# An adaLN transformer block: other places for a batch's products, GpSimd's small works and unread products, and another order at both ends

## The chip, the cores and the metric

One core of a Trainium2 chip runs the whole program. The metric is the device time of one execution in microseconds. TensorE does the matrix products, VectorE, ScalarE and GpSimd the elementwise work, SyncE's queue issues nearly all DMAs. Here GpSimd is called POOL in rows, VectorE DVE, ScalarE ACT, TensorE PE.

## The reference

Eight batches of 512 tokens, width 128, 16 heads of 8, all in f32. Only what the kernel's stages answer to is kept:

```python
mod = (silu(c) @ wmod).reshape(8, 6, 1, 128)       # sa, ca, ga, sb, cb, gb
ga = (2 * (ga >= 0) - 1) * maximum(abs(ga), 0.25)  # gb likewise
h = layernorm(x) * (1 + ca) + sa
q, k, v = split(h @ w_qkv.T)                       # 16 heads
a = q @ k.T * 8 ** -0.5
a = a - max(a, axis=-1)
s = where(a >= 0, 1 + a * (1 + a/2 * (1 + a/3)), 1 / (1 - a * (1 - a/2 * (1 - a/3))))
x = x + ga * ((s / sum(s)) @ v @ w_out.T + b_out)
h = layernorm(x) * (1 + cb) + sb
h = 2 * relu(s0 * [h, -h] @ sign(k0))              # 512 wide
h = 2 * relu(s1 * h @ sign(k1))                    # 512 wide
x = x + gb * (s2 * h @ sign(k2))
```

## The kernel before

**Steps.** The attention of all batches is one pipeline of 128 steps, 16 a batch (`b`, `n` in the code); 16 steps ahead (batch FIRST, -1) and 5 behind fill and drain it. In a step m, TensorE makes the maximum-shifted logits of group m+1 as two pairs of products into the two halves of PSUM tensor Z (`scores`, line 561), and for group m+7 unshifted logits into SA (`logits`, line 576), of which VectorE takes row maxima (line 975). ScalarE squares Z (line 720), VectorE makes a cubic of square and Z (line 966), POOL squares that (line 1201), ScalarE takes its reciprocal square root two steps later (`prob_of`, line 734): that is the unnormalised probability. Five steps behind, it is multiplied with v into OP (`with_v`, line 593); each fourth step OP is copied to OT and from there DMAs gather numerators and denominators into nd. Every fourth step (n = 1, 5, 9, 13) VectorE also does three small operations on the maxima (`of_maxima`), whose rows go to QH by eight small DMAs.

**Products in between.** All other products stand in the tables MISC (lines 68 to 97): name, which batch relative to b, and pieces (step, place, number of chunks). Places in a TensorE step (`pe_step`): scores 0, **a**, logits 1, fill, with_v, **b**, scores 1, **c**, logits 0, **d**. For batch b these are hT, q, k, v of b+1, x1, h2T and l0_0 to l0_3 of b-1, l1_0 to l1_3 and y of b-2. They share the one PSUM bank MB but for those in `own_bank`; the first chunk of each waits until the product before it has been copied out, by ScalarE (`take`, at the place of the product's last piece, after the squares or after prob), or for the late ones by VectorE (`take_late`). Batches 0 and 1 have no l1 and y, batch 0 also no x1, h2T and l0.

**Products without reader.** `fill` (line 612) multiplies ident by a block of W1 into MB in the steps of table FILL; nothing reads it. The entry names the product whose copy must be over.

**Small works.** MAIN_AT gives the steps of the work on x1: xbg (x plus gate times bias), woG (output weights times gate), den and att, the layer norm's statistics (VectorE) and root, x1n and xn (POOL; x1n of batch 6 is on VectorE, `norm_late`, line 1021). POOL splits q and k into a rounded and a rest part (`parts_of`, steps 1 and 2) and puts v in place (`v_in`).

**SyncE.** `sp_step` (line 1327) is the queue's order within a step: gate rows to gA (n = 0) and gB (n = 12), then the parts of q and k to DRAM (`write_parts`, n = 3, eight DMAs), the gates' rows (batch FIRST, n = 9), nd from OT and the rows of maxima (n = 1, 5, 9, 13), and the loads of a quad of heads from DRAM (`read_parts`, n = 2, 6, 10, 14; the first quad of the next batch at n = 6).

**The end.** After the last step `pe_tail`, `dve_tail`, `act_tail` and `pool_tail` do the rest of batch 7: the last head group is picked by two products (`pick_last`, line 598) so that it needs no DMA, then att, x1, h2T, l0, l1, y.

Of the kernel before, what the change touches and what calls it, by code (L numbers as in the profile page):

```python
# [137 lines left out]
def adaln_block(nc, x, w_qkv, w_out, b_out, k0, k1, k2, s0, s1, s2, c, wmod, out):  # L138
# [7 lines left out]
    with ExitStack() as ctx:  # L146
# [386 lines left out]
        def pe_step(pe, s):  # L533
# [64 lines left out]
            def pick_last():  # L598

                pe.wait_ge(s_pick, 2)  # L600
                pe.wait_ge(s_cv, 2 * GROUPS)
                pe.wait_ge(s_ot, B * NQ)
                for a in (1, 0):
                    nc.tensor.matmul(last_nd[:, a, :], pick[:, a, :], OT[:, (B * NQ - 1) % 2, :], start=True, stop=True)\
                        .then_inc(s_picked, 1)

# [32 lines left out]

        def pe_tail(pe):  # L640
            pe.wait_ge(t_att, 1)
            pe.wait_ge(s_wog, B)
            pe.wait_ge(s_xbg, B)
            for t in range(TB):
                to = t_x1_banks[t // 2][:, t % 2, :]
                nc.tensor.matmul(to, ident[:, :], xs[:, B - 1, t, :], start=(t % 2 == 0), stop=False, skip_group_check=True)
                nc.tensor.matmul(to, num[0:LAST, t * P:(t + 1) * P], woG[0:LAST, :], start=False, stop=False,
                                 skip_group_check=True)
# [308 lines left out]
        def dve_step(dve, s):  # L957
# [63 lines left out]
            def norm_late():  # L1021

                norm_sums()
                if at(s, "x1n", -1, b, n):
                    dve.wait_ge(s_made["h2T"], B - 2)
                    dve.wait_ge(s_rs2, B - 1)
                    for t in range(TB):
                        last = nc.vector.tensor_scalar(x1n[:, t, :], xs[:, b - 1, t, :], mv2[:, t, 0:1], rs2[:, t:t + 1],
                                                       ALU.subtract, ALU.mult)
                    last.then_inc(s_x1n, 1)  # L1030
# [405 lines left out]
```

## Time and profile before

| | us |
|---|---|
| median of 3 runs (708.7 to 710.2) | 709.76 |
| the profiled execution | 708.76 |
| its span, first to last instruction | 706.9 |
| busy: DVE | 646.2 (91%) |
| busy: PE | 627.4 (89%) |
| busy: POOL | 599.0 (85%) |
| busy: ACT | 598.8 (85%) |
| mean granted clock of TensorE | 0.971 |

The span is without what lies around the first and last instruction. All four engines are busy most of the time, so shares of the whole say little; the pipeline is read batch by batch and step by step. Cuts between batches are the starts of VectorE's cubic of a batch's first group: 40.23, 121.56, 203.43, 281.44, 359.47, 437.50, 515.54, 593.57; the one of the last group starts at 664.72. A granted clock of 1.00 is TensorE's 2.4 GHz, 0.50 is 1.2 GHz.

### The profile page before, as it was taken

How to read it: one execution, taken by the hardware profiler on the slowest of the kernel's cores; microseconds unless marked ns; L12 is line 12 of the kernel's file. 1: busy time of each engine (PE TensorE's matmuls, PEld its weight loads, DVE VectorE, ACT ScalarE, POOL GpSimd, SP SyncE). 2: the span in 40 equal slices, each digit the busy share in tenths (PEclk: the TensorE clock that was granted, in tenths of full speed). 3: DMA queues.
4: the chain of work that ended last, by engine and by line, in shares of the span. 5: the costliest groups of instructions: out<-in, count | busy, mean ns of one | idle time of the engine just before them, and what ended most of it. 6: DMA issues, size and time to landing. Idle time of an engine off the chain costs nothing.

```text
span 706.9 us, 9679 instructions
## 1 busy us (share of the span) xinstructions
PE 627.4 (89%) x3019; PEld 244.5 (35%) x3019; DVE 646.2 (91%) x768; ACT 598.8 (85%) x606; POOL 599.0 (85%) x390
## 2 busy tenths in 40 slices
PE   7577787877789999899989999899989999997798
PEld 5222222223222344233423333233423343334266
DVE  6899988989999999999999999999999999998943
ACT  2647877978899999999999989999999989998932
POOL 7769777897989999899989999899989989798920
PEclk9579999999999999999999999999999999999999
DMA  7514112141124222141224122241125112101001
GB/s 206 160 46 165 48 51 61 54 149 32 55 58 144 81 58 73 48 159 32 57 76 168 50 58 75 60 167 41 40 61 172 53 54 72 54 10 27 17 12 30
DMA packets 37783, 53.61 MB, mean 76 GB/s; under 512 B 11308, under 2 KB 20804, under 8 KB 37732
## 3 DMA queue, kind: packets, MB, share of 16 engines
q1 hardware_dynamic: 36766, 51.81, 24.1%
q10 hardware_dynamic: 966, 1.19, 0.6%
q8 instruction: 24, 0.39, 0.2%
q14 instruction: 27, 0.22, 0.1%
HBM read 29.17 MB, written 18.36 MB: 67 GB/s over the span
## 4 chain that ended last, share of the span: by engine, by line
PE 56%; DVE 17%; ACT 12%; issue 11%; POOL 2%; SPq 1%; DMA 1%; ACTq 0%; DVEq 0%; POOLq 0%
PE MB L515 13%; PE OP L593 12%; PE Z L561 9%; PE SA L576 8%; DVE cub L966 8%; DVE mx L975 7%; ACT sq L720 5%; ACT prob L734 4%; PE MB L528 3%; PE MB L505 2%; PE MB L612 2%; PE MB L486 1%; PE OP L443 1%; DVE st L1012 1%; PE MB L493 1%
## 5 line engine op out<-in xcount | busy, mean ns | idle before, releaser
L1201 POOL TENSOR_TENSOR cub<-cub 128x2048 f32<-128x2048 f32 x127 | 456.8, 3602 | 48.4 <-DVE cub L966 48.1
L720 ACT ACTIVATE sq<-Z,shift 128x1024 f32<-128x1024 f32 x256 | 282.3, 1116 | 58.5 <-PE Z L561 56.8
L966 DVE SCALAR_TENSOR_TENSOR cub<-sq,Z 128x1024 f32<-128x1024 f32 x256 | 309.8, 1211 | 13.0 <-ACT sq L720 12.2
L975 DVE TENSOR_REDUCE mx<-SA 128x2 f32<-128x1024 f32 x248 | 301.9, 1217 | 15.6 <-PE SA L576 12.2
L734 ACT ACTIVATE prob<-cub 128x2048 f32<-128x2048 f32 x128 | 244.3, 1910 | 0.4 <-PE OP L593 0.4
L576 PE MATMUL SA<-KH,QL 64*128 64x512 f32 x496 | 121.1, 485 | 33.4 <-DVE mx L975 29.3
L561 PE MATMUL Z<-QH,KH 64*128 64x512 f32 x512 | 128.8, 499 | 17.7 <-DVE cub L966 16.5
L593 PE MATMUL OP<-prob,Vq 128*16 128x512 f32 x1024 | 136.6, 607 | 0.0
L561 PEld LDWEIGHTS Z<-QH,KH 64*128 64x128 f32 x512 | 48.4, 185 | 197.6 <-DVE cub L966 121.6
L515 PE MATMUL MB<-hid,W 128*128 128x512 f32 x192 | 108.0, 645 | 0.0
L576 PEld LDWEIGHTS SA<-KH,QL 64*128 64x128 f32 x496 | 47.4, 187 | 111.1 <-DVE mx L975 89.4
L505 PE MATMUL MB<-h2T,W 128*128 128x512 f32 x56 | 31.5, 644 | 7.3 <-ACT hid L775 4.0
L515 PEld LDWEIGHTS MB<-hid,W 128*128 128x128 f32 x192 | 28.5, 188 | 23.4 <-issue 23.4
L612 PE MATMUL MB<-W,ident 128*128 128x512 f32 x54 | 33.4, 702 | 1.0 <-ACT xs L757 0.6
L593 PEld LDWEIGHTS OP<-prob,Vq 128*16 128x16 f32 x1024 | 16.9, 94 | 47.6 <-issue 42.0
L528 PE MATMUL MB<-W2G,hid 128*128 128x128 f32 x160 | 23.2, 288 | 1.3 <-ACT Vn L765 1.3
L528 PEld LDWEIGHTS MB<-W2G,hid 128*128 128x128 f32 x160 | 19.4, 191 | 6.5 <-issue 3.7
L483 PE MATMUL MB<-hT,wq 128*128 128x512 f32 x16 | 10.6, 750 | 6.8 <-ACT hT L745 6.8
L783 ACT ACTIVATE OT<-OP 128x512 f32<-128x512 f32 x28 | 16.5, 591 | 0.0
L775 ACT ACTIVATE hid<-MB,sv 128x512 f32<-128x512 f32 x24 | 16.3, 679 | 0.0
L1229 POOL TENSOR_SCALAR SQ<-SQ 128x512 fp32r<-128x512 f32 x7 | 4.3, 619 | 13.1 <-ACT SQ L754 13.1
L775 ACT ACTIVATE hid<-MB 128x512 f32<-128x512 f32 x24 | 14.4, 602 | 0.0
(205 smaller groups left out, 501.6 us busy)
## 6 DMA issues: line engine op xcount, KB each, us to landing
QL<-parts_q SPq DMA_DIRECT2D x62, 128.0 KB, 2.6
KH<-parts_k SPq DMA_DIRECT2D x62, 128.0 KB, 2.7
QH<-parts_q SPq DMA_DIRECT2D x62, 128.0 KB, 2.7
parts_q<-SQ SPq DMA_DIRECT2D x28, 256.0 KB, 2.5
parts_k<-SK SPq DMA_DIRECT2D x28, 256.0 KB, 2.7
QH<-mp SPq DMA_DIRECT2D x253, 2.0 KB
nd<-OT SPq DMA_DIRECT2D x124, 32.0 KB
out<-y SPq DMA_DIRECT2D x7, 256.0 KB, 2.8
```

Source lines behind the costliest of these rows:

```text
L505: mm = nc.tensor.matmul(bank, W0[:, m * P:(m + 1) * P], h2T[:, :], start=True, stop=True)
L515: mm = nc.tensor.matmul(bank, W1f[:, kc, m * P:(m + 1) * P], hid0[:, kc, :], start=(kc == 0), stop=(kc == KC - 1))
L528: mm = nc.tensor.matmul(bank4[:, t, :], hid1[:, kc, t * P:(t + 1) * P], W2G[:, kc, :], start=(kc == 0), stop=(kc == KC - 1))
L561: mm = nc.tensor.matmul(Z[:, h, e * S:(e + 1) * S], KH[rows, 2 * g + r, keys], QH[rows, 2 * g + r, :], start=True, stop=True)
L576: mm = nc.tensor.matmul(unit_bank(m, u)[:, e, :], QL[rows, 2 * g + r, qt * P:(qt + 1) * P], KH[rows, 2 * g + r, :], start=True, stop=True)
L593: mm = nc.tensor.matmul(OP[32 * j:32 * j + 2 * HD, :], Vq[:, tb, hh, :, :].rearrange("p d a -> p (d a)"), slot[:, tb % 2, j % 2, :], start ...
L612: nc.tensor.matmul(MB[:, :], ident[:, :], W1f[:, n % KC, :], start=True, stop=True)
L720: nc.scalar.activation(sq[:, h, :], Z[:, h, :], ACT.Square, bias=shift[:, 0:1]).then_inc(s_sq, 1)
L734: nc.scalar.activation(prob[:, m % RING, :], cub[:, m % RING].rearrange("p a n -> p (a n)"), RSQRT)\
L966: nc.vector.scalar_tensor_tensor(cub[:, m % RING, h, :], sq[:, h, :], CUB_ADD, Z[:, h, :], ALU.add, ALU.mult).then_inc(s_cv, 1)
L975: nc.vector.tensor_reduce(to, unit_bank(m, u)[:, :, :], AX_X, ALU.max).then_inc(s_mx, 1)
L1201: nc.gpsimd.tensor_tensor(ff, ff, ff, ALU.mult).then_inc(s_fp, 1)
```

## The change

The tables get other places. In the main one l1_0 comes first (steps 0 and 1), hT and q stand in step 2, k in step 3 at c, v in step 7 at d, and y fills 11c to 12d. In batch 7, l0_0 to l0_3 stand one step later at place b; in the last stage l1_3 comes first, in a bank of Z. FILL gains steps 0 and 1 and loses 3 in batches 0 and 1; in batch 1 also 12 (with another condition) and 13. xbg and woG move to steps 1 and 2 (0 at the end), parts_of to 3 and 4, write_parts to 5 and behind the other DMAs of its step, the load of gA to step 12 of the batch before, the gates' rows to step 13 behind the loads. x1n of batch 6 goes to POOL. The square of the last group goes from step 127 to 128, behind the copy to OT; pick_last goes from step 132 into the tail, behind the identity products of x1.

```diff
 MAIN = [
-    ("hT", 1, [(0, "c", 4)]), ("q", 1, [(0, "d", 4)]), ("k", 1, [(1, "d", 4)]),
-    ("l1_0", -2, [(2, "c", 1), (2, "d", 1), (3, "c", 1), (3, "d", 1)]),
-    ("l1_1", -2, [(4, "c", 1), (4, "d", 1), (5, "c", 1), (5, "d", 1)]),
-    ("l1_2", -2, [(6, "c", 1), (6, "d", 1), (7, "c", 1), (7, "d", 1)]),
+    ("l1_0", -2, [(0, "c", 1), (0, "d", 1), (1, "c", 1), (1, "d", 1)]),
+    ("hT", 1, [(2, "c", 4)]), ("q", 1, [(2, "d", 4)]), ("k", 1, [(3, "c", 4)]),
+    ("l1_1", -2, [(3, "d", 1), (4, "c", 1), (4, "d", 1), (5, "c", 1)]),
+    ("l1_2", -2, [(5, "d", 1), (6, "c", 1), (6, "d", 1), (7, "c", 1)]),
+    ("v", 1, [(7, "d", 4)]),
...
-    ("v", 1, [(11, "c", 4)]),
-    ("y", -2, [(11, "d", 1), (12, "c", 1), (12, "d", 1), (13, "c", 1)]), ("h2T", -1, [(13, "d", 4)]),
+    ("y", -2, [(11, "c", 1), (11, "d", 1), (12, "c", 1), (12, "d", 1)]), ("h2T", -1, [(13, "d", 4)]),
...
 MISC[B - 1] = [
-    ("l0_0", -1, [(11, "c", 4)]), ("l0_1", -1, [(12, "c", 4)]), ("l0_2", -1, [(13, "c", 4)]), ("l0_3", -1, [(14, "c", 4)]),
+    ("l0_0", -1, [(12, "b", 4)]), ("l0_1", -1, [(13, "b", 4)]), ("l0_2", -1, [(14, "b", 4)]), ("l0_3", -1, [(15, "b", 4)]),
...
 MISC[B] = [
-    ("l1_2", -2, [(2, "c", 4)]), ("l1_3", -2, [(4, "b", 2), (4, "c", 2)]), ("y", -2, [(5, "c", 3), (5, "d", 1)]),
+    ("l1_3", -2, [(0, "b", 3), (0, "c", 1)]), ("l1_2", -2, [(2, "c", 4)]), ("y", -2, [(5, "c", 3), (5, "d", 1)]),
...
-FILL = {(FIRST, n): ("v", 1) for n in range(13, 16)}
-FILL |= {(0, n): ("k", 2) for n in range(2, 12)} | {(0, n): ("v", 2) for n in range(12, 16)}
-FILL |= {(1, n): ("k", 3) for n in range(2, 8)} | {(1, n): ("x1", 1) for n in range(9, 12)} | {(1, 12): ("v", 3)}
+FILL = {(FIRST, n): ("v", 1) for n in range(13, 16)} | {(0, n): ("v", 1) for n in range(3)}
+FILL |= {(0, n): ("k", 2) for n in range(4, 8)} | {(0, n): ("v", 2) for n in range(8, 16)}
+FILL |= {(1, n): ("v", 2) for n in range(3)} | {(1, n): ("k", 3) for n in range(4, 8)}
+FILL |= {(1, n): ("x1", 1) for n in range(9, 14)}
...
-MAIN_AT = {"xbg": 6, "wog": 5, "den_sq": 6, "den_inv": 6, "att": 7, "st2": 9, "mv2": 10, "rs2": 11, "x1n": 11,
+MAIN_AT = {"xbg": 1, "wog": 2, "den_sq": 6, "den_inv": 6, "att": 7, "st2": 9, "mv2": 10, "rs2": 11, "x1n": 11,
-AT[B] = MAIN_AT | {"w2g": 0, "wog": 1, "xbg": 1}
+AT[B] = MAIN_AT | {"xbg": 0, "wog": 0, "w2g": 1}
...
-                    product(B, "l1_3", B - 2): (SA[:, 0, :], product(B - 1, "l1_0", B - 2)),
+                    product(B, "l1_3", B - 2): (Z[:, 1, 0:S], None),
...
         def pe_tail(pe):
+            pe.wait_ge(s_xbg, B)
+            pe.wait_ge(s_taken["l1_3"], B - 1)
+            for t in range(TB):
+                nc.tensor.matmul(t_x1_banks[t // 2][:, t % 2, :], ident[:, :], xs[:, B - 1, t, :], start=(t % 2 == 0), stop=False,
+                                 skip_group_check=True)
+            pick_last(pe)
             pe.wait_ge(t_att, 1)
...
         def dve_step(dve, s):
             if b == B - 1:
-                norm_late()
+                norm_sums()
...
-            if s == GROUPS - 1:
-                last_square(dve)
...
             if b == B and n == 0:
+                last_square(dve)
                 take_late(dve, B - 1, "l1_0")
                 take_late(dve, B - 1, "l1_1")
+                take_late(dve, B, "l1_3")
...
         def pool_step(pool, s):
-            if n in (1, 2) and 0 <= b < B:
-                parts_of(b + 1, "qk"[n - 1])
-            if n in (3, 5):
-                v_in(b, 2 if n == 3 else 3)
+            if n in (3, 4) and 0 <= b < B:
+                parts_of(b + 1, "qk"[n - 3])
+            if n in (2, 5):
+                v_in(b, 2 if n == 2 else 3)
...
-            if at(s, "x1n", -1, b, n) and b < B - 1:
+            if at(s, "x1n", -1, b, n):
                 normalise_x1(b - 1)
...
         def sp_step(sp, s):
-            if n == 0 and live(b - 1):
+            if n == 12 and live(b):
...
-            if n == 3 and live(b + 1):
+            if n == (3 if b == FIRST else 5) and live(b + 1):
...
-            if b == FIRST and n == 9:
-                sp.wait_ge(s_gate, 7)
-                sp.dma_start(gate_rows, g_row).then_inc(s_gw, 16)
+            if b == FIRST and n == 13:
+                sp.wait_ge(s_gate, 7)
+                sp.dma_start(gate_rows, g_row).then_inc(s_gw, 16)
```

The block of n = 3 / 5 in sp_step stands in front of the nd transfers and the rows of maxima before, and behind them after; the one of the gates' rows goes behind the loads.

## Rows read from the trace of the kernel before

**Rows 1.** Stretch, length, busy PE, PEld, DVE, ACT, POOL, granted clock, DMA share, GB/s.
```profile
40.23:121.56 81.33, 62.60 (x260) 20.28 (x258) 74.67 (x78) 60.80 (x51) 61.56 (x28) 0.90 0.23 73
121.56:203.43 81.87, 63.62 (x323) 21.35 (x320) 75.57 (x84) 69.68 (x63) 70.16 (x43) 0.98 0.24 72
203.43:281.44 78.01, 74.26 (x365) 27.85 (x366) 75.80 (x86) 73.80 (x70) 73.34 (x48) 1.00 0.27 82
```

**Rows 2.** Timeline, TensorE, batches 2 and 3: start, length, instruction, idle before.
```profile
283.11 1.12 PE L505 MATMUL MB<-h2T,W 128*128 128x512 f32 x2 [0.26 <-ACT hid L775]
...
285.81 0.50 PE L561 MATMUL Z<-QH,KH 64*128 64x512 f32 x2
...
288.29 1.10 PE L483 MATMUL MB<-hT,wq 128*128 128x512 f32 x2 [0.96 <-ACT hT L745]
...
290.96 0.51 PE L561 MATMUL Z<-QH,KH 64*128 64x512 f32 x2
...
300.51 0.50 PE L561 MATMUL Z<-QH,KH 64*128 64x512 f32 x2
...
305.22 0.50 PE L561 MATMUL Z<-QH,KH 64*128 64x512 f32 x2
```

**Rows 3.** Waits: engine line waited for, us in total, times, longest.
```profile
PEld MB L498 <- ACT y L761: 2.9, 5, 0.6
PEld MB L528 <- ACT Vn L765: 2.9, 5, 0.6
```

**Rows 4.** Timeline, SyncE's queue and TensorE, batch 3.
```profile
304.50 2.56 SPq L409 DMA_DIRECT2D parts_k<-SK  x4
...
310.51 4.34 SPq L435 DMA_DIRECT2D QH<-mp  x8
...
325.67 0.50 PE L576 MATMUL SA<-KH,QL 64*128 64x512 f32 x2
```

**Rows 5.** DMA issues: count, KB each, median us to landing.
```profile
parts_k<-SK SPq DMA_DIRECT2D x28, 256.0 KB, 2.7
...
KH<-parts_k SPq DMA_DIRECT2D x62, 128.0 KB, 2.7
```

**Rows 6.** Busy time of one stretch, columns as in Rows 1.
```profile
45.10:55.40 10.30, 8.85 (x19) 3.18 (x20) 8.69 (x11) 5.38 (x7) 8.52 (x6) 0.50 0.10 27
```

**Rows 7.** Timeline, TensorE, batches 0 and 1.
```profile
113.43 2.07 PE L612 MATMUL MB<-W,ident 128*128 128x512 f32 x2
...
117.06 0.50 PE L561 MATMUL Z<-QH,KH 64*128 64x512 f32 x2
...
183.29 0.51 PE L561 MATMUL Z<-QH,KH 64*128 64x512 f32 x2
...
187.06 1.13 PE L612 MATMUL MB<-W,ident 128*128 128x512 f32 x2
...
189.10 0.50 PE L561 MATMUL Z<-QH,KH 64*128 64x512 f32 x2
```

**Rows 8.** Timeline, SyncE's queue, head.
```profile
20.41 2.69 SPq L409 DMA_DIRECT2D parts_q<-SQ  x4
26.05 0.32 SPq L1358 DMA_DIRECT2D gate_rows<-prob  x1
```

**Rows 9.** Timeline, GpSimd, VectorE and ScalarE, batch 7.
```profile
641.77 3.60 POOL L1201 TENSOR_TENSOR cub<-cub 128x2048 f32<-128x2048 f32 x1
...
643.07 2.38 DVE L1028 TENSOR_SCALAR x1n<-xs,mv,rs 128x128 f32<-128x128 f32 x1
...
646.14 1.21 DVE L966 SCALAR_TENSOR_TENSOR cub<-sq,Z 128x1024 f32<-128x1024 f32 x1
...
650.76 0.77 ACT L769 ACTIVATE h2T<-MB,mod 128x512 f32<-128x512 f32 x1
```

**Rows 10.** Timeline, TensorE, tail.
```profile
679.31 1.90 PE L604 MATMUL Z<-OT,pick 128*32 128x512 f32 x4
...
684.05 1.15 PE L652 MATMUL Z<-woG,nd 32*128 32x128 f32 x8
```

More of the change, by code:

```diff
@@ L473, in misc_product @@
                 pe.wait_ge(s_mx, 2 * GROUPS)
+            elif first and b == B:
+                pe.wait_ge(s_cv, 2 * GROUPS)
             bank4 = bank.rearrange("p (t d) -> p t d", t=TB)
@@ L596, in with_v @@
                 mm.then_inc(s_pv, 1)
[L598 to L605, printed above, removed]
             def fill():
@@ L620, in pe_step @@
             misc("b")
-            if s == B * H - 1 + AV_BEHIND:
-                pick_last()
             scores(s + 1, 1)
@@ L638, in adaln_block, with pick_last @@
         t_y_banks = [tiles_of(Z[:, 0, 0:S]), tiles_of(Z[:, 0, S:2 * S])]
-        def pe_tail(pe):
+        def pick_last(pe):
+            pe.wait_ge(s_pick, 2)
+            pe.wait_ge(s_cv, 2 * GROUPS)
+            pe.wait_ge(s_ot, B * NQ)
+            for a in (1, 0):
+                nc.tensor.matmul(last_nd[:, a, :], pick[:, a, :], OT[:, (B * NQ - 1) % 2, :], start=True, stop=True)\
+                    .then_inc(s_picked, 1)
+        def pe_tail(pe):
+            pe.wait_ge(s_xbg, B)
[4 more added lines that the diff above has]
+            pick_last(pe)
             pe.wait_ge(t_att, 1)
             pe.wait_ge(s_wog, B)
-            pe.wait_ge(s_xbg, B)
             for t in range(TB):
[L645 to L648, printed above, removed]
+                nc.tensor.matmul(t_x1_banks[t // 2][:, t % 2, :], num[0:LAST, t * P:(t + 1) * P], woG[0:LAST, :],
+                                 start=False, stop=False, skip_group_check=True)
             pe.wait_ge(s_att, B)
@@ L1019, in norm_sums @@
                     bn.then_inc(s_mv2, 1)
[L1021 to L1030, printed above, removed]
             m = s + AHEAD
@@ L1074, in dve_tail @@
             nc.vector.tensor_tensor(num[LAST:P], last_nd[:, 0, :], den[LAST:P], ALU.mult).then_inc(s_att, 1)
-            take_late(dve, B, "l1_3")
             dve.wait_ge(s_x1n, B - 1)
@@ L1328, in sp_step @@
             b, n = s // H, s % H
-            if n == 0 and live(b - 1):
-                if b == 1:
+            if n == 12 and live(b):
+                if b == 0:
                     sp.wait_ge(s_gw, 16)
-                need(sp, s_xbg, b - 1)
-                sp.dma_start(gA[:, :], gate_rows[b - 1:b, 0:2 * D].partition_broadcast(P)).then_inc(s_gA, 16)
+                need(sp, s_xbg, b)
+                need(sp, s_wog, b)
+                sp.dma_start(gA[:, :], gate_rows[b:b + 1, 0:2 * D].partition_broadcast(P)).then_inc(s_gA, 16)
             if n == 12 and live(b - 1) and b < B:
@@ L1337, in sp_step @@
                 sp.dma_start(gB[:, :], gate_rows[b - 1:b, 2 * D:3 * D].partition_broadcast(P)).then_inc(s_gB, 16)
-            if n == 3 and live(b + 1):
+            quad, tb = (s - 1 - AV_BEHIND) // QUAD, (s - 1 - AV_BEHIND) % QUAD
+            if 0 <= quad < B * NQ and tb == TB - 1:
+                beta, g = quad // NQ, quad % NQ
+                sp.wait_ge(s_ot, quad + 1)
+                if g == 0:
+                    need(sp, s_made["x1"], beta)
+                for j in range(QUAD if quad < B * NQ - 1 else 0):
+                    r = 32 * g + HD * j
+                    sp.dma_start(nd[r:r + HD, :, :], OT[32 * j:32 * j + 2 * HD, quad % 2, :]).then_inc(s_gat[quad % 2], 16)
+            if (s + AHEAD - 4) % QUAD == 0 and 0 <= s + AHEAD - 4 < GROUPS:
+                quad = (s + AHEAD - 4) // QUAD
+                g = quad % NQ
+                sp.wait_ge(s_mp, quad + 1)
+                need(sp, s_z, 8 * (quad - NQ + 1))
+                rows_of_maxima(sp, quad, 0, range(P // 32))
+                rows_of_maxima(sp, quad, 1, range(P // 32 if quad else 1))
+            if n == (3 if b == FIRST else 5) and live(b + 1):
                 beta = b + 1
```

16 lines of the change are left out of this document (removed).

## The prediction

> **What bounds the kernel now.** First the stretches by batch, each cut at the first cubic of its batch (VectorE, line 966) [rows 1]. Batch 2 takes 78.01 us with VectorE busy 75.80, TensorE 74.26, ScalarE 73.80 and GpSimd 73.34, at a granted clock of 1.00 (2.4 GHz). Batches 2 to 6 repeat this, so whatever changes in a step of theirs counts five times. Batches 0 and 1 have fewer products (no l1, no y) and yet take 81.33 and 81.87, with VectorE busy 74.67 and 75.57: 6.7 and 6.3 us of VectorE's time are idle there, where batch 2 has 2.2. The slack is in batches 0 and 1; in the others only a stall of TensorE can be won or lost.
>
> How a stall arises is seen in TensorE's order [rows 2]. A step holds two pairs of score products (Z), two pairs of logits (SA), the product with v, and one misc chunk at place c and one at d. With both filled it lasts 4.71 (Z at 300.51 to Z at 305.22). Nearly all misc products share bank MB, so one that starts at d right after another has ended at c waits for ScalarE's copy: 0.26 between l0_2 and l0_3 (283.11). Where hT stands at c and q at d, q waits 0.96 (288.29) and the step lasts 5.15 (285.81 to 290.96). In the list of waits, y behind v and h2T behind y (both c to d) cost 2.9 us each in five times, 0.6 a time [rows 3].
>
> **The change part by part.**
>
> *Steady batches.* Removed are two c-to-d pairs, v/y and y/h2T, 1.2 a batch by [rows 3]. Added are k/l1_1 (step 3), l1_1/l1_2 (step 5) and l1_2/v (step 7). The nearest row for them gives 0.26, for a plain copy out of the same bank [rows 2]; two of the three copy with a scale, and the last meets a ScalarE that has just done the two den operations of step 6. So I take 0.3, 0.4 and 0.6, together 1.3; bounds 0 (all absorbed) and 1.8 (0.6 each, as [rows 3]). The hT/q pair keeps its 0.96 but leaves step 0, where OT's copy stands on ScalarE too. The empty place moves from 1c to 13c, ahead of VectorE's three small operations on the maxima, which set that step's length anyway: I charge 0.1 for that. Sum +0.2 a batch, **+1.0** for five, between -4 and +4. GpSimd's small works only trade places (the parts of q and k to steps 3 and 4, xs with the gate to step 1, woG to step 2). ScalarE uses a square two steps after it is made; that hides them, and I cost them at nothing. Without this cover the 1.7 to 2 us of each would stand in its step.
>
> *SyncE's queue.* write_parts moves from step 3 to step 5, behind four nd transfers and eight rows of maxima. Those rows are issued from 310.51 for 4.34, to 314.85 [rows 4]. Four k writes take 2.56, and the q writes as much: issued 314.9 to 320.0. The last k write lands 2.7 after its issue at about 319.4, so KH's two halves are read from 322.1 and 322.7, and the second lands 2.7 later, at 325.4 [rows 5]. TensorE's first logits of the next batch, which need it, stand at 325.67, and after the change about 0.5 later [rows 4]. It fits by some 0.8 us: cost 0, bounds 0 and 1.2 a batch (each of the two landings that it hangs on one microsecond longer than here). Queued behind it are only QH's reads, needed seven steps later. The two gA loads and gate_rows trade places where nobody waits, but for the head, below.
>
> *Batch 0.* A granted clock of 0.90 over 81.33 us means 16 us at 0.50 (1.2 GHz) [rows 1]; 10.30 of them are one stretch from 45.1 on [rows 6], the rest two short ones. The long one lies on steps 1 and 2, and in steps 0 and 1 there is no product without reader. VectorE is busy 8.69 of its 10.30, so it costs 1.6. With fills in steps 0 to 2 I take all of it off: -1.6, bounds 0 and -2. A short one costs what fill and product with v lose: from fill to the next Z 3.63 (113.43 to 117.06) against 2.04 (187.06 to 189.10), 1.6 [rows 7]. The two here and the one in batch 1 (0.98 over 81.87) lie in steps that have a fill before and after; I leave them. v at 11c with a fill in the next step makes a chain in which nothing fills the wait for the maxima: 5.81 (183.29 to 189.10) [rows 7]. At 7d it does fill it, and the step is about 4.6: -1.2, bound 0. Sum **-2.8**.
>
> *Batch 1.* The same -1.2 for v, but k at 3c with a fill in step 4 now forms that chain, +1.2. The fill that had to wait for k's copy is gone, and so is what hT/q, OT and VectorE's small operations cost when they met in steps 0 and 1: I take -0.6 for both, a third of the 1.2 and 0.6 above; bounds +1 and -2. Sum **-0.6**.
>
> *Head.* gate_rows is issued at 26.05, ahead of the loads of quad 1, for whose KH TensorE then stands idle. After the change it follows them. The q writes before it are issued until 23.1 [rows 8] and land, at the 2.7 of [rows 5], only near 25.7, so **-0.4** and not more; bounds 0 and -1.
>
> *Batch 7.* x1n leaves VectorE, where it fills the 3.07 from 643.07 to the cubic at 646.14 [rows 9]. On GpSimd it can start only as the square ends, at 645.37, and takes about 2.3 with its two small steps: ready near 647.7 instead of 646.1, and h2T (10d) waits for it. But cubic and ScalarE's squares before h2T run earlier, and h2T is copied near 649 instead of 650.76. l0 one step later at place b keeps up with that. I take **-1.9**; bounds 0 (all lost in waiting for x1n) and -3.1. The first of x1n's four instructions takes 2.38 and ends as GpSimd's square does; the other three are through by 646.14. **The Trainium skill**, SBUF — State Buffer, section "Who interferes with whom", has it that a VectorE tensor_scalar in a two-port mode and a GpSimd instruction shut each other out, and the one that issues second blocks fully. By that rule some 2.3 of the 3.07 are the block and 0.8 the work, so an x1n on VectorE that met no square would cost 0.8, and the term could not be larger than here; the trace agrees as far as the 2.38 goes.
>
> *Tail.* l1_3 leaves step 4 of the last stage, and the identity products come ahead of pick. From pick's start to the products that need the last att there are 4.74 us (679.31 to 684.05), 1.90 of them pick [rows 10]; the other 2.84 are half of l1_3 and eight identity and woG products. They go before pick or under its last att, which takes two ScalarE operations and one VectorE operation behind pick's first half; my estimate from pick's start to the end of that is 3.0. So -1.7. l1_3's 2.1 us of products in step 0, and the last square behind OT's copy, push the last product with v back by 0.8. Sum **-0.9**, bounds +1 and -2.
>
> **Sum** against the profiled execution's 708.76: +1.0 - 2.8 - 0.6 - 0.4 - 1.9 - 0.9 = -5.6, 703.2. The median of the runs is 1.0 above that execution, hence 704.2; I give **704.0**.
>
> **The rivals.** (a) *The clock still falls.* The early steps hold a single fill each, steps 3 and 8 none, and the short falls came in steps that had one. If the long stretch comes back (1.6) and one more short one (1.6), the time is 707.2. Against it: batch 2, with two chunks a step, shows none. (b) *The falls vanish altogether*, since v and k leave the steps in which TensorE stood idle and bunched its work: 3 x 1.6 less, 699.2. Against it: steps 8 to 15 of batch 0 hold the same fill as before. (c) *Slower: KH comes late in every batch.* SyncE's queue is now full from 307 to 324. The gain is eaten if logits wait 0.8 in each of seven batches, that is, if the k writes and the read behind them take 1.6 more than 5.4 together; with 2.0 more it is 712.4. For it: reads now follow 2 MB of writes directly; against it: these are the medians of transfers issued just as densely. (d) *Nothing gained but batch 0:* the three new pairs cost 0.6 each (+2.5), and x1n gives nothing back (+1.9): 708.4.
>
> **How the numbers follow.** Main forecast 0.56, (a) 0.18, (b) 0.12, (c) 0.08, (d) 0.06. A measurement of this kernel tells a difference from none at about 0.2%, 1.4 us. Main, (a) and (b) are faster by more; (d) with the edge of (a) and (c) makes 0.06 within it; slower are most of (c) and a little of (d). Faster 0.86, same 0.06, slower 0.08. The range goes from (b) to (d): 699.0 to 708.6.
>
> **What would show it.** Right: batch 0 near 78.5, batch 1 near 81.3, batches 2 to 6 at 78.2, the long stretch at low clock gone, quad 1's loads issued near 26.0, no x1n on VectorE in batch 7, about 3 us from pick to the products with the last att. Wrong: a wait of TensorE for KH at step 8 of each batch; batches 2 to 6 off by more than 0.5 each (then the prices of the pairs are wrong); low clock in new places.

## The result and the profile after

The changed kernel takes **714.1 us** (median of 9 runs, 713.22 to 723.1) against 709.76 (9 runs, 706.82 to 711.35): ratio 1.0098, 95% interval 1.0061 to 1.0136. It is slower by 1%; 704.0 was forecast, and "faster" had 0.86. The profiled execution took 714.03, span 711.7, 4.8 longer than the span before (706.9).

Stages, each cut at the first cubic of its batch (us; "g10" and "g15" are the cubics of groups 10 and 15 of batch 7):

| stage | before | after | change | forecast |
|---|---|---|---|---|
| start to batch 0 | 40.23 | 39.18 | -1.05 | -0.4 |
| batch 0 | 81.33 | 79.82 | -1.5 | -2.8 |
| batch 1 | 81.87 | 81.95 | +0.1 | -0.6 |
| batches 2 to 6 | 390.14 | 393.98 | +3.8 | +1.0 |
| batch 7 to g10 | 48.36 | 48.37 | 0 | } -1.9 |
| batch 7, g10 to g15 | 22.79 | 28.45 | +5.7 | } |
| g15 to the end | 42.22 | 39.98 | -2.2 | -0.9 |

The stretches of the profile after that answer to [rows 1], and g10 to g15:

```profile
39.18:119.00 79.82, 60.84 (x263) 19.91 (x262) 74.75 (x77) 60.39 (x51) 61.34 (x28) 0.95 0.23 73
119.00:200.95 81.95, 65.77 (x327) 22.04 (x324) 75.76 (x85) 69.88 (x63) 70.49 (x43) 0.98 0.24 74
200.95:279.81 78.86, 74.03 (x365) 27.71 (x366) 75.95 (x85) 74.00 (x70) 73.05 (x48) 1.00 0.25 79
643.29:671.74 28.45, 21.69 (x104) 8.44 (x102) 17.11 (x18) 21.04 (x17) 22.56 (x12) 0.88 0.09 24
```

The same stretch g10 to g15 of before, not shown so far:

```profile
641.93:664.72 22.79, 17.41 (x100) 7.43 (x98) 19.80 (x23) 20.25 (x16) 19.17 (x6) 1.00 0.11 29
```

Read the last rows against each other: VectorE has 2.7 us less to do and yet the stretch is 5.7 longer, TensorE's busy time is up by 4.3 with four matmuls more, and the granted clock is 0.88 instead of 1.00. No engine is full: they wait for each other, at 1.2 GHz for part of it.

In steps 12 to 14 of batch 7 VectorE does, in this order: the two cubics of a group, in step 12 the copy of OP to OT, then the copy of l0_j in two instructions (QL<-MB, written by `take_late` in step 12+j), then the next group's cubics. TensorE, VectorE and ScalarE there, timeline of after (start, length, instruction, idle before):

```profile
651.12 0.50 PE L564 MATMUL Z<-QH,KH 64*128 64x512 f32 x2
...
654.27 0.51 PE L564 MATMUL Z<-QH,KH 64*128 64x512 f32 x2 [2.66 <-DVE cub L970]
...
654.72 1.91 PE L596 MATMUL OP<-prob,Vq 128*16 128x512 f32 x8
...
656.55 1.85 PE L508 MATMUL MB<-h2T,W 128*128 128x512 f32 x2
...
656.69 0.69 DVE L942 COPY OT<-OP 128x512 f32<-128x512 f32 x1 [1.34 <-PE OP L596]
...
658.34 0.50 PE L564 MATMUL Z<-QH,KH 64*128 64x512 f32 x2
658.44 0.69 DVE L952 TENSOR_SCALAR QL<-MB 128x512 fp32r<-128x512 f32 x1 [1.06 <-PE MB L508]
658.88 1.11 ACT L724 ACTIVATE sq<-Z,shift 128x1024 f32<-128x1024 f32 x1 [2.10 <-PE Z L564]
...
659.77 2.34 DVE L970 SCALAR_TENSOR_TENSOR cub<-sq,Z 128x1024 f32<-128x1024 f32 x2
...
665.23 0.69 DVE L952 TENSOR_SCALAR QL<-MB 128x512 fp32r<-128x512 f32 x1 [3.12 <-PE MB L508]
...
666.57 2.34 DVE L970 SCALAR_TENSOR_TENSOR cub<-sq,Z 128x1024 f32<-128x1024 f32 x2
...
670.41 0.69 DVE L952 TENSOR_SCALAR QL<-MB 128x512 fp32r<-128x512 f32 x1 [1.50 <-PE MB L508]
```

and of before:

```profile
651.67 1.10 PE L505 MATMUL MB<-h2T,W 128*128 128x512 f32 x2 [0.80 <-ACT h2T L769]
...
652.57 2.35 DVE L966 SCALAR_TENSOR_TENSOR cub<-sq,Z 128x1024 f32<-128x1024 f32 x2 [1.65 <-ACT sq L720]
...
653.84 0.49 PE L561 MATMUL Z<-QH,KH 64*128 64x512 f32 x2 [1.07 <-DVE cub L966]
654.27 1.05 PE L593 MATMUL OP<-prob,Vq 128*16 128x512 f32 x8
...
655.25 0.50 PE L561 MATMUL Z<-QH,KH 64*128 64x512 f32 x2
...
655.39 0.69 DVE L938 COPY OT<-OP 128x512 f32<-128x512 f32 x1 [0.47 <-PE OP L593]
656.00 0.68 DVE L948 TENSOR_SCALAR QL<-MB 128x512 fp32r<-128x512 f32 x1
...
657.32 2.34 DVE L966 SCALAR_TENSOR_TENSOR cub<-sq,Z 128x1024 f32<-128x1024 f32 x2
...
659.58 0.68 DVE L948 TENSOR_SCALAR QL<-MB 128x512 fp32r<-128x512 f32 x1
```

Before, l0_0 is made at 651.67, in a gap, long ahead of VectorE's copy of it at 656.00, and only the product with v (1.05) stands between the two halves of the scores of a group: 653.84 to 655.25, 1.41. After, the gap is empty (2.66 idle), and then both the product with v (1.91) and l0_0 (1.85) stand between the halves: 654.27 to 658.34, 4.07.

VectorE does its cubics, comes to the copy of l0 and waits there, in step 13 for 3.12, since TensorE makes l0 only behind the first half of the scores and the product with v of the same step. The next cubics follow the copy without idle time, so it is this wait that sets the step, not ScalarE's square of the second half. VectorE's idle time in steps 12, 13 and 14 is 2.40 (1.34 for the product with v and 1.06 for l0), 3.12 and 1.50; before it is 0.47, 0 and 0.14. That is 6.4 more, and the three steps together are 6.6 longer.

Steps 10 to 14 take 4.14, 5.57, 6.78, 6.79, 5.18; before 5.34, 5.29, 4.75, 3.59, 3.81. The clock falls for 3.4 us each from 654.6 and from 661.5; step 14, from 666.57 on, is wholly at 2.4 GHz.

Waits of after, which answer to [rows 3] and have no counterpart there:

```profile
PEld MB L489 <- ACT hid L779: 4.4, 5, 0.9
PEld MB L518 <- ACT hid L779: 3.3, 5, 0.7
PEld SA L579 <- DMA KH<-parts_k: 3.2, 5, 1.0
...
PEld MB L518 <- ACT SK L758: 2.9, 5, 0.6
```

The first is v behind l1_2, the second l1_2 behind l1_1, the fourth l1_1 behind k: the three new pairs. The third is the wait for KH at step 8. The queue in batch 3, as [rows 4]:

```profile
308.95 4.70 SPq L436 DMA_DIRECT2D QH<-mp  x8
313.77 2.52 SPq L410 DMA_DIRECT2D parts_q<-SQ  x4
316.34 2.56 SPq L410 DMA_DIRECT2D parts_k<-SK  x4
318.99 1.19 SPq L426 DMA_DIRECT2D QL<-parts_q  x2
321.10 1.08 SPq L426 DMA_DIRECT2D KH<-parts_k  x2
```

Counted from the start of its batch, the KH read is issued at 41.3 (321.10 less 279.81), where 40.7 was forecast (322.1 less 281.44). The median landing of the k writes went from 2.7 to 3.3:

```profile
parts_k<-SK SPq DMA_DIRECT2D x28, 256.0 KB, 3.3
```

Tail and x1n of after:

```profile
647.28 1.74 POOL L1198 TENSOR_SCALAR x1n<-xs,rs,nm 128x128 f32<-128x128 f32 x4
...
685.62 1.90 PE L638 MATMUL Z<-OT,pick 128*32 128x512 f32 x4
...
688.80 1.15 PE L656 MATMUL Z<-woG,nd 32*128 32x128 f32 x8 [0.19 <-DVE nd L1067]
```

3.18 from pick to the products with the last att, where [rows 10] has 4.74; 3.0 was estimated.

### The profile page after: what moved, and what is told of

Its sections match the earlier page's. It is cut to its first block, busy times and chain, and to the rows that moved or that the text cites. A ratio compares the mean times of both kernels' runs of the same rounds, so it can differ in the third digit from the quotient of the medians.

```text
span 711.7 us, 9704 instructions
## 1 busy us (share of the span) xinstructions
PE 628.5 (88%) x3025; PEld 243.8 (34%) x3025; DVE 642.9 (90%) x764; ACT 599.5 (84%) x606; POOL 598.7 (84%) x396
## 4 chain that ended last, share of the span: by engine, by line
PE 49%; DVE 14%; ACT 11%; issue 10%; SPq 10%; DMA 5%; POOL 1%; ACTq 0%; DVEq 0%; POOLq 0%
PE OP L596 11%; PE Z L564 8%; PE MB L518 8%; PE SA L579 6%; DVE cub L970 6%; DVE mx L979 6%; ACT sq L724 4%; SPq L410 4%; ACT prob L738 3%; PE MB L508 3%; SPq L436 3%; DMA parts_k<-SK 3%; DMA KH<-parts_k 2%; PE MB L531 2%; PE MB L486 2%
## 5 line engine op out<-in xcount | busy, mean ns | idle before, releaser
L579 PE MATMUL SA<-KH,QL 64*128 64x512 f32 x496 | 119.1, 476 | 34.9 <-DVE mx L979 29.7
L606 PE MATMUL MB<-W,ident 128*128 128x512 f32 x60 | 37.5, 709 | 1.9 <-ACT Vn L769 1.2
L508 PE MATMUL MB<-h2T,W 128*128 128x512 f32 x56 | 33.0, 673 | 3.6 <-ACT hid L779 3.6
L486 PE MATMUL MB<-hT,wq 128*128 128x512 f32 x16 | 8.8, 630 | 7.1 <-ACT hT L749 7.1
```

The lines of the kernel that those rows point to most:

```text
L508: mm = nc.tensor.matmul(bank, W0[:, m * P:(m + 1) * P], h2T[:, :], start=True, stop=True)
L579: mm = nc.tensor.matmul(unit_bank(m, u)[:, e, :], QL[rows, 2 * g + r, qt * P:(qt + 1) * P], KH[rows, 2 * g + r, :], start=True, stop=True)
L606: nc.tensor.matmul(MB[:, :], ident[:, :], W1f[:, n % KC, :], start=True, stop=True)
```

## The experiments

Fourteen kernels, all computing the whole reference. "Start" is the kernel that is edited. Ratios are to the kernel before on the same chip.

| label | start | median us | ratio | 95% interval | mean of batches 3 to 6 | g10 to g15 |
|---|---|---|---|---|---|---|
| l0_back | after | 711.87 | 1.0057 | 1.0028 to 1.0085 | 78.81 | 24.89 |
| x1n_vector | after | 720.44 | 1.0193 | 1.0151 to 1.0235 | 78.96 | 30.37 |
| q_written_at_4 | after | 714.89 | 1.0109 | 1.0077 to 1.0142 | 78.44 | 28.34 |
| end_only | before | 707.12 | 1.0003 | 0.9973 to 1.0032 | 78.0 | 22.79 |
| l0_late | before | 713.74 | 1.0092 | 1.0062 to 1.0122 | 78.0 | 30.36 |
| x1n_gpsimd | before | 707.03 | 0.9977 | 0.9943 to 1.0012 | 78.0 | 21.88 |
| fills_0_1 | before | 710.62 | 1.0035 | 1.0002 to 1.0069 | 78.0 | 22.79 |
| v_at_13c | q_written_at_4 | 710.58 | 1.0029 | 1.0005 to 1.0053 | 78.24 | 29.45 |
| l0_at_a | before | 715.09 | 1.0100 | 1.0064 to 1.0136 | 78.0 | 28.35 |
| parts_kept | before | 705.64 | 0.9948 | 0.9920 to 0.9976 | 78.0 | 21.88 |
| more_fill | parts_kept | 703.47 | 0.9924 | 0.9899 to 0.9949 | 78.0 | 21.88 |
| after_fill_11 | after | 713.80 | 1.0075 | 1.0041 to 1.0109 | 79.37 | 28.36 |
| at_a_fill_11 | l0_at_a | 712.69 | 1.0064 | 1.0043 to 1.0085 | 78.0 | 27.59 |
| at_a_fill_all | l0_at_a | 712.78 | 1.0064 | 1.0043 to 1.0085 | 78.0 | 27.00 |

The last two columns come from one profiled execution each. Those of x1n_gpsimd (715.10), q_written_at_4 (720.06), v_at_13c (718.73) and after_fill_11 (722.15) were 5 to 8 us longer than their medians, with more falls of the clock. In batches 3 to 6 only after_fill_11 has a fall, one in batch 5.

**l0_back**: l0 where it was.

```diff
-    ("l0_0", -1, [(12, "b", 4)]), ("l0_1", -1, [(13, "b", 4)]), ...
+    ("l0_0", -1, [(11, "c", 4)]), ("l0_1", -1, [(12, "c", 4)]), ...
```

> The changed kernel with l0_0 to l0_3 of batch 7 back at 11c, 12c, 13c, 14c; all else as changed. Theory (the loss of batch 7 is l0's place: VectorE takes l0_j in step 12+j ahead of the next step's cubics, and TensorE now makes it only in that step, so each waits for the other): the stretch from the cubic of group 10 to that of group 15 of batch 7, 28.5 us in the changed kernel and 22.8 before, falls to 21 to 22.5, the two short falls of the clock there vanish, total 706.5 to 708. Rival (x1n on GpSimd makes h2T late and that starves the end): the stretch stays above 26, total above 711.

Neither theory's number: the stretch fell from 28.45 to 24.89, where 21 to 22.5 or above 26 had been named, and the total, 711.87, is the rival's. But a fall of the clock of 10.2 us is still in the stretch; without one it is 21.88 (parts_kept), which is the theory's. The tail went from 39.98 to 41.11, so part of the gain was paid back there.

**x1n_vector**: x1n of batch 7 back on VectorE, all else as after.

> The changed kernel with x1n of batch 6 back on VectorE; l0 stays at place b one step later. Theory (l0's place): steps 12 to 14 of batch 7 stay near 18.7 us (6.8, 6.8, 5.2), steps 10 and 11 go from 9.7 to 10.6, total 714 to 716. Rival (x1n): steps 12 to 14 return to about 12.2, total near 708.

Slower still, 720.44. With l0 late, x1n on VectorE costs 1.9 in the stretch (30.37 against 28.45): 0.9 in steps 10 and 11, as much as the move gave by itself (x1n_gpsimd), and 1.0 in steps 12 and 13, which here were almost wholly at 1.2 GHz (7.29 and 7.27). The rest of the 6 us between the medians is not in these stages of one execution: its runs spent 54.6 us at 1.2 GHz on average, those of after 43.3 (twice the clock's shortfall from 1, times the span). The row, VectorE in batch 7:

```profile
644.86 3.15 DVE L1037 TENSOR_SCALAR x1n<-xs,mv,rs 128x128 f32<-128x128 f32 x4
```

GpSimd's square ran there from 643.55 for 3.60, to 647.15, and x1n ended 0.86 after it, as in [rows 9]. **The Trainium skill**, SBUF — State Buffer, section "Who interferes with whom", says the later of two such instructions blocks fully; both traces agree.

**q_written_at_4**: the q writes one step before the k writes.

```diff
+            if n == 4 and b >= 0 and live(b + 1):
+                ...
+                write_parts(sp, "q", b + 1)
...
-                    write_parts(sp, "q", beta)
                     write_parts(sp, "k", beta)
```

> The changed kernel with the four q writes issued in step 4, when SyncE's queue is free, and only the four k writes in step 5. Theory (KH of the next batch is late because all eight writes stand behind nd and the rows of maxima): the wait of TensorE for KH (3.2 us in five times) vanishes, step 9 of batches 2 to 6 goes from a mean of 6.24 to 5.75 and of batch 0 from 6.35 to 5.2 to 5.4; total -3 to -4, near 710.5. Rival (the new pairs of products at c and d make the batches longer, KH hardly): step 9 changes by less than 0.2, total within 1 of the changed kernel.

No wait of TensorE for KH is left in the batches. Batches 3 to 6 take 78.44 instead of 78.78 (the same four of after): KH cost **0.34 a batch**. The other 0.41 above 78.03 is the products' places. The whole kernel didn't gain: 714.89, with 710.5 expected. Its runs spent 49.8 us at 1.2 GHz on average, those of after 43.3, and in the profiled one batches 0 to 2 took 85.03, 83.64 and 80.03. Whether the earlier writes have a part in these falls is not shown.

**v_at_13c**: the kernel above with v in the empty place 13c (and six products without reader of batch 0 waiting for k's copy instead of v's, which stands later now).

```diff
-    ("v", 1, [(7, "d", 4)]),
+    ... ("y", ...), ("v", 1, [(13, "c", 4)]), ("h2T", -1, [(13, "d", 4)]),
```

> The changed kernel with the q writes in step 4 and with v at 13c, the empty place, instead of 7d. Theory (a c-to-d pair costs what the copy leaves over, and l1_2/v behind the den operations 0.6 to 0.9): the steps 7 and 8 of batches 3 to 6 (5.28 and 4.87) go to about 5.0 and 4.55; the new pair v/h2T gives 0.5 back in 13 and 14; batches 3 to 6 from 78.44 to 78.2 to 78.5. Rival (the steps are set by ScalarE's den operations, not by the pair): steps 7 and 8 stay, batches longer by 0.5.

78.24 a batch: the l1_2/v pair is worth 0.34 in step 8 and 0.19 in step 9 (5.90 to 5.71), and v/h2T takes 0.3 of it back in step 14 (4.52 to 4.83). Step 7 stays at 5.29, where 5.0 was expected: its length is not v's.

**end_only**: the kernel before with the order of the last stage of after (l1_3 in its step 0, identity products ahead of pick, the last square after OT).

```diff
-    ("l1_2", -2, [(2, "c", 4)]), ("l1_3", -2, [(4, "b", 2), (4, "c", 2)]), ("y", -2, ...
+    ("l1_3", -2, [(0, "b", 3), (0, "c", 1)]), ("l1_2", -2, [(2, "c", 4)]), ("y", -2, ...
...
-            if s == B * H - 1 + AV_BEHIND:
-                pick_last()
```

> The kernel before with the other order after step 127 alone: l1_3 first and in a bank of Z, last square behind OT's copy, identity products of x1 ahead of pick, gate works first on GpSimd. l0, x1n and all tables of batches 0 to 7 as before. If the tail's gain is its own: from the first cubic of the last group to the end 42.2 us become 40.0 to 41.3 (forecast in the prediction: -0.9), total -1 to -2. If it was a gift of the late batch 7: 42 or more, no difference.

The tail is 41.17 instead of 42.22, -1.05 with -0.9 forecast. The median doesn't show it (1.0003): runs scatter by more than that.

**l0_late**: l0 at place b of the next step, in the kernel before (the reverse of l0_back's diff).

> The kernel before with only l0_0 to l0_3 of batch 7 one step later, at place b. Theory (l0's place alone makes batch 7 slow): group 10 to group 15 of batch 7 goes from 22.8 to 28 to 30.5 us, total +5 to +7. Rival (it is slow only with x1n on GpSimd or with the other order at the end): below 25, total +2 at most.

30.36 instead of 22.79, the only edit: **+7.6**, low clock for 13.7 us from 651.9. This alone makes the kernel 1.0092 (four runs), near the 1.0098 of the whole change; the change's other losses and gains nearly cancel. Steps 12 and 13 are 7.28 and 7.27 here, with VectorE idle for 2.90 and 3.60 at its copies. The tail is longer too, 43.35 instead of 42.22, with a fall of 3.4 us in it.

**x1n_gpsimd**: x1n of batch 7 on GpSimd, in the kernel before (and the reverse of this for x1n_vector).

```diff
             if b == B - 1:
-                norm_late()
+                norm_sums()
...
-            if at(s, "x1n", -1, b, n) and b < B - 1:
+            if at(s, "x1n", -1, b, n):
                 normalise_x1(b - 1)
```

> The kernel before with only x1n of batch 6 on GpSimd. From the pair changed kernel / x1n back on VectorE (28.5 against 30.4 us) it would gain 1.9; from the pair kernel before / changed kernel with l0 back (22.8 against 24.9, with 10 us at the low clock) it would lose 2.1. Theory: a gain of 1 to 2 where the clock stays high; the loss comes with the stretch of low clock from 655 on. Rival: h2T behind GpSimd's square costs it whatever the clock: 24 to 25.

-0.91 in the stretch; -1.9 was forecast for it. The ratio, 0.9977, can't be told from 1. This run shows something else too. Its batch 1 has the code of before, and took 88.71 instead of 81.87, with the same busy time of VectorE (75.70 against 75.57 in [rows 1]) and the clock at 0.87:

```profile
121.53:210.24 88.71, 71.51 (x322) 24.51 (x318) 75.70 (x85) 70.22 (x62) 71.03 (x43) 0.87 0.24 71
```

**fills_0_1**: products without reader in steps 0 and 1 of batches 0 and 1 only.

```diff
-FILL = {(FIRST, n): ("v", 1) for n in range(13, 16)}
+FILL = {(FIRST, n): ("v", 1) for n in range(13, 16)} | {(0, 0): ("v", 1), (0, 1): ("q", 2), (1, 0): ("v", 2), (1, 1): ("q", 3)}
```

> The kernel before with products without reader added in steps 0 and 1 of batches 0 and 1. As the prediction had it: the stretch of low clock at 45 us vanishes or shrinks to 3.4, mean low time of the runs 6 to 7 us less than that of the kernel before (37), total -2. Rival (one fill a step keeps no clock up; a fall comes wherever it meets the three small operations of VectorE): low time within 3 us of before, total within 1.

Batch 0 took 77.75, batch 1 88.60, with falls of the clock at 143.4, 163.9 and 177.5. Over all runs the time at 1.2 GHz is 38.4 us of the span against 41.0 in before (reckoned as for x1n_vector), and the kernel isn't faster. Two fills a batch don't hold the clock, and in the time they can't be told from none or a small loss.

**l0_at_a**: l0 one step late, but ahead of the product with v, so that VectorE's copy doesn't wait for it.

```diff
-    ("l0_0", -1, [(11, "c", 4)]), ...
+    ("l0_0", -1, [(12, "a", 4)]), ...
```

> The kernel before with l0_0 to l0_3 of batch 7 at place a of steps 12 to 15, half a step before place b (l0_late, 30.4 us from group 10 to 15). Theory (l0_j has to be made before VectorE has done the cubics of step 12+j, since its copy stands between them and the next step's): at a it is made while the second cubic runs, so most of the loss is gone: 23 to 25 us. Rival (one step late is too late for l1's chunks and for bank MB, wherever in the step it stands): 28 or more.

**A miss.** 28.35, the rival's number; step 12 alone took 7.91. VectorE's rows:

```profile
657.28 0.69 DVE L938 COPY OT<-OP 128x512 f32<-128x512 f32 x1 [3.63 <-PE OP L593]
657.89 0.68 DVE L948 TENSOR_SCALAR QL<-MB 128x512 fp32r<-128x512 f32 x1
...
662.61 0.69 DVE L948 TENSOR_SCALAR QL<-MB 128x512 fp32r<-128x512 f32 x1 [1.06 <-PE MB L505]
```

The wait didn't go, it moved. In step 12 VectorE copies OP to OT ahead of l0, and the product with v now stands behind l0. In step 13 l0 at place a is still made too late for its copy, by 1.06. What the two can't tell apart is how much the clock does, which fell from 651.1 on for 6.8 us, while TensorE stood idle for 2.97 behind the empty place of step 11.

**after_fill_11** and **at_a_fill_11**: a product without reader where l0_0 used to be.

```diff
             scores(s + 1, 1)
             misc("c")
+            if (b, n) == (B - 1, 11):
+                pe.wait_ge(s_taken["h2T"], B - 1)
+                nc.tensor.matmul(MB[:, :], ident[:, :], W1f[:, n % KC, :], start=True, stop=True)
```

> The kernel after with one product more, without reader, into MB in step 11 of batch 7 at place c, where the kernel before had l0_0 and TensorE now stands idle for 2.66 us (651.62 to 654.27 of the profile after). Nothing else is changed; l0 stays one step late. Theory C (the emptiness of step 11 costs: the clock falls there, and the product with v and l0 of the next steps run at 1.2 GHz, 1.91 and 1.85 instead of 1.05 and 1.1): no fall of the clock near 654, steps 12 and 13 take about 5.2 instead of 6.8, groups 10 to 15 about 25.0 instead of 28.45. Theory D (the order alone costs: VectorE's copy of l0 waits for a product that stands behind the product with v, and the next product waits for VectorE): groups 10 to 15 stay at 27.5 or more, steps 12 and 13 at 6.3 or more, with or without the fall. Both can be partly so: what is above 22.8 at full clock is the order's.

28.36. The product stood in step 11, and the clock fell in step 12 all the same (product with v 1.69, l0 2.08); steps 12 and 13 took 6.77 and 6.69, with VectorE waiting 1.30 and 3.02 for l0. The fill shortened TensorE's idle time in step 11 (0.40 before it, 1.14 behind it, instead of 2.66) and did not keep the clock up, so theory C's forecast failed and D's holds for this kernel.

> The kernel before with l0_0 to l0_3 at place a of steps 12 to 15 (as in l0_at_a) and the same product without reader in step 11 of batch 7. Theory C: without a fall of the clock at 651 the 7.91 of step 12 goes back to 5 to 5.3, groups 10 to 15 take 23 to 24.5 instead of 28.35, close to the 22.79 of the kernel before, since VectorE waits for no product at place a. Theory D: they stay at 27 or more.

27.59, theory D's number. But step 12 ran wholly at 2.4 GHz:

```profile
653.38 0.50 PE L561 MATMUL Z<-QH,KH 64*128 64x512 f32 x2 [1.14 <-DVE cub L969]
653.81 1.13 PE L505 MATMUL MB<-h2T,W 128*128 128x512 f32 x2
...
654.87 1.05 PE L593 MATMUL OP<-prob,Vq 128*16 128x512 f32 x8
655.85 0.51 PE L561 MATMUL Z<-QH,KH 64*128 64x512 f32 x2
...
655.99 0.69 DVE L941 COPY OT<-OP 128x512 f32<-128x512 f32 x1 [1.53 <-PE OP L593]
...
657.92 2.34 DVE L969 SCALAR_TENSOR_TENSOR cub<-sq,Z 128x1024 f32<-128x1024 f32 x2
...
659.18 0.80 PE L561 MATMUL Z<-QH,KH 64*128 64x512 f32 x2 [2.83 <-DVE cub L969]
659.91 2.07 PE L505 MATMUL MB<-h2T,W 128*128 128x512 f32 x2
```

2.47 between the halves instead of 1.41, the step 5.81 instead of 4.75: 1.06 longer at full clock, what l0 (1.13) adds. The step is set by VectorE, whose copy to OT waits 1.53 for the product with v instead of 0.47, also 1.06 more, and whose next cubic (657.92) follows its copies without idle time. TensorE then stands 2.83 idle for VectorE's cubic and comes back at 1.2 GHz.

**at_a_fill_all**: the same product at place c of steps 12 to 14 too.

> at_a_fill_11 with the product without reader at place c in steps 12, 13 and 14 of batch 7 too (each waits for VectorE's copy of that step's l0, since both are in MB). The fills only keep TensorE busy. at_a_fill_11 showed step 12 at full clock: 5.81 us against 4.75 in the kernel before, the first half of the scores to the second half 2.47 against 1.41, because l0 stands between the two halves. Theory E (both causes, in about equal parts): the clock doesn't fall between groups 10 and 15, steps 12, 13, 14 take 5.8, 4.3 and 4.5 against 4.75, 3.59, 3.81, groups 10 to 15 about 25.2: 2.4 of the 4.8 lost in at_a_fill_11 were the order's, the rest the clock's. Rival F (the clock alone; step 12 was a single case): 23 to 24. Rival G (the order alone): 27 or more at full clock.

27.00; steps 12, 13, 14 took 5.81, 5.43, 5.12. The clock fell once more, for 3.4 us from 656.7, in step 13. The gap ahead of it was not filled: the product without reader had to wait for VectorE's copy of l0.

```profile
655.74 1.15 PE L628 MATMUL MB<-W,ident 128*128 128x512 f32 x2 [1.71 <-DVE QL L954]
656.86 0.79 PE L561 MATMUL Z<-QH,KH 64*128 64x512 f32 x2
657.59 2.07 PE L505 MATMUL MB<-h2T,W 128*128 128x512 f32 x2
659.59 1.29 PE L593 MATMUL OP<-prob,Vq 128*16 128x512 f32 x8
```

Scores, l0 and the product with v took 0.79, 2.07 and 1.29 here instead of 0.50, 1.13 and 1.05, together 1.5 more. Steps 12 and 14, at full clock, are 1.06 and 1.31 longer than before, but the fill of step 13 (1.13, at 661.24) stands ahead of the scores of step 14 and has a part in the 1.31. Rival F, the clock alone, is out. Between E and G the run doesn't decide, since both spoke of the full clock; 27.00 less 1.5 is 25.5, near E's 25.2, if all of the 1.5 counted.

**parts_kept**: the kernel before with what had shown a gain alone: end order, x1n on GpSimd, and gate_rows issued in step 13 of the first stage.

```diff
-            if b == FIRST and n == 9:
+            if b == FIRST and n == 13:
                 sp.wait_ge(s_gate, 7)
                 sp.dma_start(gate_rows, g_row).then_inc(s_gw, 16)
```

> The kernel before with the three parts of the change that the runs so far show as gains: the order of the end, x1n on GpSimd, gate_rows behind the loads in step 13. At equal time at the low clock: tail -1.05, batch 7 -0.9, head -0.4, together -2.3, so 706 where the kernel before has 708.4. Rival (x1n and the tail take the same slack): -1.3 or less.

705.64, ratio 0.9948 with an interval below 1: a little faster than the kernel before, and so than the change; -2.7 against the kernel before on its chip, -2.3 expected. Its profiled span is 700.4, 11.3 below that of after.

**more_fill**: the kernel above with half products without reader (256 columns) at place d in batches 0 and 1.

```diff
+FILL_D = {(0, n): ("k", 2) for n in range(3, 11)} | {(0, n): ("v", 2) for n in range(12, 16)}
+FILL_D |= {(1, n): ("k", 3) for n in range(3, 8)} | {(1, n): ("x1", 1) for n in range(9, 11)} | {(1, 12): ("v", 3)}
...
             misc("d")
+            ...
+                nc.tensor.matmul(MB[:, 0:256], ident[:, :], W1f[:, n % KC, 0:256], start=True, stop=True)
```

> parts_kept with a second product without reader of half the width (256 columns) at place d in the steps 3 to 10 and 12 to 15 of batch 0 and 3 to 7, 9, 10 and 12 of batch 1. If it is only too little work of TensorE that lets the clock fall there: no fall in these steps, mean low time from 41 to 27 to 30 us, total 4 below parts_kept, batch 0 near 77, batch 1 near 79.5. Rival (the falls come from the waits in steps 0, 1, 8 and 11, or the extra product costs as much as it saves): low time less by under 5, total within 1.5.

703.47, ratio 0.9924, the lowest of all, but its interval overlaps that of parts_kept, so a gain by the fills isn't shown; 4 had been expected, or under 1.5 by the rival. Its runs spent 33.8 us at 1.2 GHz on average, parts_kept's 41.0 and before's 40.2. A straight line through the runs of a kernel gives 0.25 to 0.41 us of span for a microsecond at 1.2 GHz, in each kernel with ten runs or more. By it, 7 fewer would be worth about 2.5 (an estimate), near the 2.2 that the medians differ by; but the runs of either kernel differ among themselves by 20 us and more of such time, so the 7 are not clear of chance either. The profiled execution shows no gain: batches 0 and 1 took 80.29 and 82.59, in parts_kept 79.13 and 81.85.

## Why the prediction was wrong

**Batch 7: the step that failed.** "l0 one step later at place b keeps up with that. I take -1.9; bounds 0 ... and -3.1." It was +5.7, outside the bounds and with the other sign. It was one sentence with no row and no price behind it, on the part of the change that decided.

Two things were missed. First, l0's place was judged by when its input is ready and not by when its reader comes: VectorE copies l0_j in step 12+j, right behind that step's cubics and ahead of the next ones. The rows of before would have given the price. From the first cubic of step 12 (652.57) the cubics take 2.35; the first half of the scores starts 1.27 after it (653.84) and the product with v 1.70 after it (654.27), so that l0 (1.13) behind that product would be ready some 3.8 after it. By this estimate VectorE waits 1.5 in each step without a copy to OT, and 0.4 in step 12, where that copy comes first. Step 14 of after, at full clock, shows it: a wait of 1.50 for l0, and 5.18 instead of 3.81.

Second, the clock falls in steps 12 and 13, behind idle times of TensorE of 2.66 and 2.20, and there the product with v and l0 take 1.91 and 1.85 to 1.89 instead of 1.05 and 1.13, 1.6 more a step. The order is worth 0.4, 1.5 and 1.4, the clock 3.2, together 6.5; measured is +6.6 in after (28.45 less the 21.88 of x1n_gpsimd and parts_kept). In l0_late, where nearly the whole of both steps was at 1.2 GHz, it is +7.6. The split is an estimate for steps 12 and 13: no run has l0 at place b and the whole stretch at full clock.

x1n itself gained 0.9, half of the forecast: from the cubic of g10 to the copy of h2T it is 7.90 in after (643.29 to 651.19) and 8.83 before (641.93 to 650.76 of [rows 9]).

**Batches 2 to 6.** Forecast +1.0, measured +3.8, within the bounds of -4 and +4. KH was costed at nothing with 0.8 to spare; it cost 0.34 a batch, 1.7 in five. The mechanism of rival (c) came, at under half its size: the k writes landed 0.6 later than the row of before and used up the spare. The products' places cost +0.41 a batch (q_written_at_4) instead of +0.2, and the nearness hides larger errors that cancel. Step by step against before: steps 3 to 5 +0.63 and steps 7 to 9 +0.84, where the three new pairs had been priced at 1.3 together; steps 13 and 14 only -0.56 for the two pairs removed, priced at 1.2; and step 1 -0.52, which the sum did not have at all. "The last meets a ScalarE that has just done the two den operations", priced at 0.6, is worth 0.53 (0.34 + 0.19).

**Batches 0 and 1.** Forecast -3.4, measured -1.4 in the profiled pair. The long stretch at 1.2 GHz from 45.1 is gone, as forecast, but short falls stand at 36.8, 47.1 and 111.9, and one of batch 1 at 132.4. That is rival (a), the clock still falls, in part: short falls in new places, but not its long stretch. The error behind it: one execution's falls were taken as places of the kernel. Of eight executions whose batches 0 and 1 have the code of before, seven take 161.0 to 163.3 for both and one takes 170.6 (x1n_gpsimd). The four with the code of after take 161.8, 162.3, 161.9 and 167.9 (after, l0_back, x1n_vector, after_fill_11), 163.5 in the mean where the eight have 163.3. So even the -1.4 is not shown to be the change's: the forecast's term is smaller than what moves by itself. Rival (b), no falls left, is refuted by every run.

**Head and tail.** The head is -0.55 in the mean (39.00 in six executions with the start of after, 39.55 in eight with that of before), near the -0.4 forecast; but the two groups overlap (37.99 to 39.44 and 38.95 to 40.23), and the profiled pair's -1.05 is part chance. Quad 1's loads were issued at 23.73, not at the 26.0 forecast, since the q writes stood there at 18.79 and not at 20.41. With gate_rows' new place alone, parts_kept and more_fill have 37.97 and 38.12; why that is shorter than after's 39.00 wasn't followed. The tail's order gives -1.05 against -0.9. The further -1.2 of after comes only with l0 late and everything else of after (39.96 to 40.00 in after, x1n_vector, q_written_at_4, v_at_13c and after_fill_11; 41.11 with l0 back); l0_late has 43.35 and l0_at_a 42.09, so l0 late by itself doesn't give it. Its cause wasn't followed.

**Where the time went.** From the profiled execution of parts_kept to that of after, batches 2 to 6 cost 3.9, g10 to g15 6.6, head 1.2, batches 0 and 1 0.8, and the tail gives 1.2 back; together 11.3. The stages fill the span, so the sum must come out; what it shows is that g10 to g15 is the largest part. Rival (d), nothing gained but batch 0, was too mild: it had no case in which batch 7 loses. What stays open: how the clock's falls could be kept out of batch 7 with l0 late, and so the measured share of the clock there.

## What to carry to other kernels

When a product is moved, ask not only when its operands are ready, but when its reader comes to it, and what stands ahead of it on its own engine in that step. The same 1.1 us of work let VectorE run on without idle time where it was made behind the second half of the scores, ahead of the step of its copy; made half a step later it cost 1.4 at full clock in step 14. And when an edit removes a wait, look whether it has only moved to the instruction before, as in l0_at_a. Price every moved instruction from a row, above all the one of which it is only said that it keeps up. And where one profile shows falls of the clock, look at the granted clock of several executions before giving their places a price.
